# Gathered graph rows summed in TensorE as three bf16 parts in place of fp32, in five stages of a four-layer graph network

## The reference, cut to what matters

```python
# layer 0: hyperbolic map of h, sum over edges, map back
support_t = segment_sum(xt[s], r, num_segments=N)
# layer 1: attention with 4 heads, then a 25-step spiking unit
e_exp = exp(e - e_max[dst]); denom = segment_sum(e_exp, dst)
alpha = e_exp / (denom[dst] + 1e-16)
out = segment_sum(xw[src] * alpha[:, :, None], dst)
# layer 2: four edge types, both directions
aggA = segment_sum(xs * m, dst); aggB = segment_sum(xd * m, src)
# layer 3: two weighted graph convolutions with layer norms
out = segment_sum(h[s] * norm[:, None], d) + b
```

## Time and profile before

| what | value |
|---|---|
| median of 3 runs | 10845.83 us (10836.53 to 10870.07) |
| the profiled execution | 10801.95 us |
| its span | 10800.2 us |
| busy: PE, PE's weight loads | 3382.4 us (31%), 2822.0 us (26%) |
| busy: DVE | 3243.6 us (30%) |
| busy: ACT | 1293.5 us (12%) |
| busy: POOL | 5734.5 us (53%) |
| mean traffic of HBM | 48 GB/s |

### The profile page before, as it was taken

The page is one execution under the profiler, slowest core; times in us unless marked ns, Lnnn a source line. Parts: engine busy times, 40 slices in busy tenths (PEclk is TensorE's granted clock), DMA queues, the critical chain, the costliest instruction groups (busy, mean ns, idle before and its releaser), DMA issues.

```text
span 10800.2 us, 102943 instructions
## 1 busy us (share of the span) xinstructions
PE 3382.4 (31%) x14814; PEld 2822.0 (26%) x14815; DVE 3243.6 (30%) x6808; ACT 1293.5 (12%) x2852; POOL 5734.5 (53%) x5941
## 2 busy tenths in 40 slices
PE   1333431000011113653443333333333333233332
PEld 1333320000011102630233333333333333233332
DVE  5334662000020002579511111111132222422224
ACT  1000012332310000137300000000000000000000
POOL 0666754555567775000266666656645665356664
PEclk6555555555555555655656665555555555555555
DMA  1111113333320001210211111111111111111111
GB/s 43 43 42 40 44 33 85 102 102 101 102 54 13 13 11 38 81 41 1 69 54 53 51 52 46 42 41 42 42 40 41 42 42 41 36 41 43 42 43 41
DMA packets 334881, 521.48 MB, mean 48 GB/s; under 512 B 120787, under 2 KB 187175, under 8 KB 334815
## 3 DMA queue, kind: packets, MB, share of 16 engines
q0 software_dynamic: 186368, 330.08, 12.3%
q1 hardware_dynamic: 148447, 190.78, 5.8%
HBM read 421.31 MB, written 99.13 MB: 48 GB/s over the span
## 4 chain that ended last, share of the span: by engine, by line
issue 27%; another core or an unknown queue 20%; PE 13%; DVE 12%; DVEq 11%; ACTq 5%; ACT 4%; DMA 1%; POOL 1%; POOLq 0%; SPq 0%
PE PS L689 12%; DVEq L302 3%; DVE OH L1201 3%; DVE OH L1195 2%; DVEq L307 2%; ACTq L56 2%; ACT SCR L926 1%; ACT EQ L930 1%; DVE T L1043 1%; DVEq L1201 1%; ACTq L302 1%; DVEq L54 1%; DVEq L1250 1%; DVEq L304 1%
## 5 line engine op out<-in xcount | busy, mean ns | idle before, releaser
L689 PE MATMUL PS<-GATHERED,OH 128*128 128x128 f32 (+1 forms) x10240 | 2421.4, 418 | 4073.1 <-DVE OH L1195 1576.4
L582 POOL DMA_INDIRECT GATHERED<-row_tab,IDX x2496 | 2456.9, 984 | 1897.3 <-issue 1021.0
L689 PEld LDWEIGHTS PS<-GATHERED,OH 128*128 128x128 f32 x10240 | 2156.2, 313 | 4385.1 <-issue 1777.5
L582 POOL DMA_INDIRECT GATHERED<-typed_tab,IDX x832 | 839.5, 1009 | 1499.3 <-ACT IDX L867 1040.4
L582 POOL DMA_INDIRECT GATHERED<-gat_tab,IDX x832 | 785.2, 944 | 743.2 <-ACT IDX L871 357.7
L582 POOL DMA_INDIRECT GATHERED<-typed_b_tab,IDX x832 | 801.0, 963 | 500.6 <-issue 246.4
L607 POOL DMA_INDIRECT list_dram<-REC_NOW,PLACE_NOW x832 | 824.3, 991 | 335.0 <-issue 281.1
L1201 DVE TENSOR_SCALAR OH<-IOTA,DSTF,WF 128x128 f32 x2048 | 603.5, 364 | 761.5 <-issue 731.0
L689 PE MATMUL PS<-T,OH 128*128 128x132 f32 x2048 | 472.5, 412 | 1134.6 <-issue 475.9
L689 PEld LDWEIGHTS PS<-T,OH 128*128 128x128 f32 x2048 | 424.9, 307 | 1182.2 <-issue 631.7
L1217 DVE TENSOR_TENSOR X<-X,PS 128x128 f32 x512 | 146.6, 286 | 1685.6 <-remote 1118.5
(11 more groups left out here) (262 smaller groups left out, 3093.8 us busy)
## 6 DMA issues: line engine op xcount, KB each, us to landing
gat_rows<-GATHERED SPq DMA_DIRECT2D x208, 264.0 KB
GATHERED<-gat_rows SPq DMA_DIRECT2D x208, 264.0 KB
GATHERED<-row_tab,IDX POOLq DMA_INDIRECT x2496
ROWI<-dst_rows SPq DMA_DIRECT2D x208, 128.0 KB
GATHERED<-gat_tab,IDX POOLq DMA_INDIRECT x832
list_dram<-REC_NOW,PLACE_NOW POOLq DMA_INDIRECT x832
GATHERED<-typed_tab,IDX POOLq DMA_INDIRECT x832
GATHERED<-typed_b_tab,IDX POOLq DMA_INDIRECT x832
```

The source lines that it names most:

```text
L582: pool.indirect_dma_start(out=rows, out_offset=None, in_=table, in_offset=bass.IndirectOffsetOnAxis(ap=IDX[:, k:k + 1], axis=0),).then_inc ...
L689: last = mm(bank(p)[:, 0:r.shape[1]], onehot(p, t), r, start=(t == 0), stop=(t == CT - 1))
```

## The change

In gb, l2, l2b, l3a and l3b the rows are split into three bf16 parts whose sum is the fp32 row, and PE makes 12 bf16 products for a sum in place of four fp32 ones. One-hots of these walks are written as bf16. The parts lie in a new tile PARTS, two chunks deep. ACT copies the row as bf16 (`hi`), DVE subtracts that from the row in place (`rest`), ACT copies what is left as bf16 (`mid`), and DVE subtracts once more into the third part (`low`). The instruction for `low` also releases the row buffer, which now happens ahead of the addition of the chunk before; PARTS is released after the addition. In l3a and l3b the edge weights are multiplied into the gathered rows, two chunks ahead, and no longer into the one-hots. In gb the weighing and the exponent go two chunks ahead in place of one. Walks share counting semaphores (`like`, `turn`). l0 and the score walk compute as before.

```diff
+        OHB = OH[:, :].bitcast(BF16)
+        PARTS = sb("PARTS", [P, 2 * CT * NP3 * XW], BF16)
...
             def gather(wk, c, u, table, width, tiles=range(CT)):
                 hold(pool, wk.free, c + 1)
-                hold(pool, wk.idx, c + 1)
+                hold(pool, wk.idx, c + (wk.turn * NCH + 1))
...
                 for t in range(CT):
-                    r = rows(t)
-                    last = mm(bank(p)[:, 0:r.shape[1]], onehot(p, t), r, start=(t == 0), stop=(t == CT - 1))
+                    parts = rows(t)
+                    for n, r in enumerate(parts):
+                        last = mm(bank(p)[:, 0:r.shape[1]], onehot(p, t, 1, r.dtype == F32), r, start=(t == 0 and n == 0),
+                                  stop=(t == CT - 1 and n == len(parts) - 1))
...
+            def split_rows(name):
+                return lambda i, u: hold(pe, walks[name].free, RING * i + (RING + 1 + u))
+            def part_rows(u, t, width=D):
+                return [parts_of(u, width)[:, k, t, :] for k in range(NP3)]
...
-            aggregate("gb", lambda i, u: hold(pe, v_made, RING * i + (u + 1 + RING)),
-                      lambda u, t: VX[:, u * CT + t, :])
+            aggregate("gb", split_rows("gb"), lambda u, t: part_rows(u, t, XW))
...
+            def high_and_middle(wk, c, u, source, ready, value):
+                hold(act, parts_free, c + (wk.split * NCH + 1))
+                hold(act, ready, value)
+                width = source.shape[2]
+                nc.scalar.activation(parts_of(u, width)[:, 0, :, :], source, ACT.Copy).then_inc(part_hi, 1)
+                hold(act, part_rest, c + (wk.split * NCH + 1))
+                nc.scalar.activation(parts_of(u, width)[:, 1, :, :], source, ACT.Copy).then_inc(part_mid, 1)
...
+                    def weigh_row(c, u, landed):
+                        hold(dve, wk.gathered[u], landed)
+                        v.tensor_tensor(rows(u), rows(u), per_edge(per_row, c, D), ALU.mult).then_inc(row_weighed, 1)
...
+                def rest(c, u):
+                    a = rows(u)
+                    hold(dve, part_hi, c + (wk.split * NCH + 1))
+                    v.tensor_tensor(a, a, parts_of(u, a.shape[2])[:, 0, :, :], ALU.subtract).then_inc(part_rest, 1)
+                def low(c, u):
+                    a = rows(u)
+                    hold(dve, part_mid, c + (wk.split * NCH + 1))
+                    v.tensor_tensor(parts_of(u, a.shape[2])[:, 2, :, :], a, parts_of(u, a.shape[2])[:, 1, :, :],
+                                    ALU.subtract).then_inc(wk.free, 1)
...
-                            onehots(c + 1, block_values((u + 1) % sets)[2], 1 - p, weights, column).then_inc(wk.onehot, 1)
+                            if not exact:
+                                rest(c + 1, (u + 1) % RING)
+                            onehots(c + 1, block_values((u + 1) % sets)[2], 1 - p, weights, column, exact).then_inc(wk.onehot, 1)
+                            if not exact:
+                                low(c + 1, (u + 1) % RING)
...
-                        dve.nop(nofuse=True).then_inc(wk.free, 1)
+                        dve.nop(nofuse=True).then_inc(wk.free if exact else parts_free, 1)
```

More of the change, by code:

```diff
@@ L885, in indices @@
                     start += n
+                if wk.split is not None:
+                    for u in range(RING):
+                        chunk(NIT - 1, u, True)
             for req in requests["before_l0"]:
```

108 lines of the change are left out of this document (77 added, 31 removed).

## The result

The changed kernel takes 11604.41 us (median of 3 runs, 11540.36 to 11613.89) against 10845.83 us: a ratio of 1.0694, 95% interval 1.0657 to 1.073. The profiled execution took 11604.41 us, and its span is 802.5 us longer than the one before.

What follows compares the result with a forecast made beforehand. The prediction took instructions and hand-overs per chunk beside POOL's indirect transfers, not busy time, as the bound. Terms 200 + 83 + 0 = +283 us gave 11085 us for the profiled execution, about 11125 with 44 added; 8-in-10 range 10350 to 11700.

Steps and rivals of the forecast that it cites:

- likeliest case: Whole kernel: more instructions in the walks and gb bound by DVE; 10950 to 11400 us, chance 0.46.
- blocked rival: Walks: more instructions than pass in a burst, a second pause each ring round; 7.0 us a chunk, 11660 us, chance 0.10.
- the chunks of gb: Sign in gb after the last scatter: chunks start 3.7 to 4.7 us apart, with DVE busy over 75%.
- the wait for the release: Sign in l2b: POOL's groups show more idle time under the buffer release than 246 us.
- the spans of l2b and l3a: Sign in two walks: l2b should span 1310 to 1380 us, l3a 1200 to 1410 us.
- gb, +200 us: gb: DVE-bound chunks of 4.2 us after the scatters, +125 us; 18 fewer chunks done beside them, +75 us.
- l2 and l2b, +83 us: Walks l2 and l2b: added instructions and hand-overs cost 0.2 us a chunk over 416 chunks, +83 us.
- l3a and l3b, 0: Walks l3a and l3b: fewer DVE instructions and early release against weighing two chunks ahead; 0, within -200 to +200 us.
- the one on PE: Walks: PE's shorter sums save 0.4 us of a mostly idle engine, worth 0 since POOL's 5.0 us cover it.
- Lengthened gathers, 0: Edited walks: DVE's two-input operations lengthen gathers, but POOL has 1.2 us a chunk of waiting to give; 0.
- The pause-free regime: Walks: long DVE operations or the early release end POOL's pauses; 10600 to 10700 us, at best about 10350, chance 0.36.
- a case of no difference: Walks: stalls go by loop passes, not instructions, so walks stay at 1300 us; within 30 us of 10846, chance 0.08.

Runs made afterwards that it cites:

- e10: The changed kernel with PARTS four chunks deep in place of two, so that ACT's first copy need not wait for an addition: 11569.97 us.
- e1c: The changed kernel with PE multiplying only the first part, 4 products a sum in place of 12: 10951.63 us, 1.017 of the kernel before.

## Why the prediction was wrong in size

The side was right (0.56 for slower), but the loss was 759 us where 279 were forecast. 11604 us lies outside the likeliest case's own 10950 to 11400, and also outside what the bounds of its terms add up to (10806 to 11451). It lies in the wide range only because that range ran to the blocked rival. Of the signs that were named, the chunks of gb (4.01 us apart, DVE busy over 75%), PE's sum (1.44 us), the gathers (1.013 us) and the wait for the release (319 us) came; the spans of l2b and l3a (1405 and 1424 us) came out above their bounds. Term by term, against the profiled execution:

- **gb, +200 us: held.** l2 starts 190 us later. DVE replaced PE as the bound, with 4.01 us a chunk where 4.2 was taken; 23 fewer chunks were done beside the scatters where 18 were. The late part is 166 x 4.01 against 143 x 3.29 us. It was PE's records that cost the 23 chunks, the second of the two measures that the prediction gave (43 chunks by PE's; 42 came). By the same measure the spare products should leave 31, and 31 came.
- **l2 and l2b, +83 us: +292.** **l3a and l3b, 0: +285.** This is where it failed, and the step is the one on PE: "In the walks this saves 0.4 us of an engine that is idle 60% of the time: worth 0". PE's time per sum was right (1.44 us for 12 products, 1.5 taken). But its records, 16 to 24 a sum, got a price of their own only in gb. In l2 and l2b they went into one count with the instructions of DVE and ACT, and that count was priced by the score walk, which has half of l2b's products (1024 against 2040) and so could not show what PE's cost; in l3a and l3b they were left out. The runs showed in its place that eight products of a sum cost some 430 us in the four walks (e10 against e1c), while hand-overs and the work of ACT and DVE cost 29 us there, and at most some 160.
- **Lengthened gathers, 0:** they are 42 us of the 112 us that l2b lost. In the run of spare operations gathers of 982 and 1002 ns cost nothing, so what they cost where POOL pauses is not settled.
- **The pause-free regime (0.36)** did not come by the change; it came with the chip, and there the change is slower too (1.0545). **The blocked regime (0.10)** came closest with its 11660 us and 7.0 us a chunk (l3b: 7.0), but that was luck, as its form did not come: two pauses of POOL in a round of 16 gathers stand in only 10 of 52 rounds of l2b (1 before) and 8 of l3b (24 before). What grew is the one pause.
- **The rule of the Trainium skill** on fetched windows ("Runtime: NRT & Kernel Launch", instruction fetch mechanics) was put down as a case of no difference, as the branches stay the same in number. The walks changed, so it does not give the time in that form. Whether fetching is what PE stands still for, no record here says. That of the same skill on two-input operations of DVE ("SBUF — State Buffer", who interferes with whom) says that they hold up only GpSimd operations that read SBUF. A gather reads its row numbers from IDX, a tile in SBUF, so the rule does not speak against the 1.21 us of gathers that start during such an operation, or against the 2.42 us of the earlier trace rows.

Open: why PE's signals come late beside POOL's transfers and only on some chips; why in the walks the price rises so little up to 8 products and so much up to 12; and whether it is larger with the split beside it than alone. Each of these walks' numbers rests on one execution.

## What to carry to other kernels

Where a stream of indirect transfers runs on GpSimd and the others show "issue" and "remote" idles, price what an edit adds to each engine's instruction stream, and not only busy time: here PE was busy for less and the kernel 7% slower. Price each engine's stream by itself, from a stage in which that engine has as much to do, and in every stage with the same condition. Run the kernel before on the same chip, twice, before a difference of 1% is believed. And hold a long stream of scatters back until the short-instruction stage beside it is done, if a stage of few, long operations can cover it.

## What the runs showed of the hardware

- One kernel took 8446 to 8461 us on two chips and 10704 to 10898 us on others, at granted clocks of 0.54 and 0.55. On the first two, the 832 gathers of the score walk come 1.25 us apart without one pause; on the others 82 to 87 pauses of over 1 us stand among them, 311 to 382 us in sum.
- In l2b of the kernel before, on the chip of the first profile, 72 of 208 additions of DVE start over 1 us after PE's last product, at most 14.5 us; in 67 of these the semaphore that PE raises is recorded just as late. In the changed kernel 83 are late, 81 with such a record. Without pauses all 208 semaphores are recorded 0.01 us after the last product, and no addition is later than 0.2 us. With four products, with pauses, 46 additions are late, 172 us in sum and at most 5.8.
- Beside POOL's scatters the chips with pauses let 552 to 656 product records of PE through in some 1110 us, whether a sum has 8, 12 or 17 of them. A chunk of gb takes 17 to 19 us in the kernel before, 26 to 28 with 12 products, and 3.3 us after the scatters.
- A gather that starts during a two-input, 512-column operation of DVE (0.69 us) takes 1.21 us in the mean and up to 1.46 in place of 0.94. One that starts while DVE does nothing is not lengthened, also beside a copy of ACT.
